# Five steps for a tile, and a second half of whole turns: the order of the later tiles and of the weights in a two-half mixture of experts

## The chip, the cores and the metric

One core of one Trainium2 chip. The metric is the time of one execution on the device in microseconds, the median of three runs. 1 per cent of it is 2.66 us.

## The reference

The input `x` has 16 sequences of 64 tokens with 256 channels: 1024 tokens. The layer norm of `x` gives the keys of a recurrent attention, the context gives its values. A scan over each sequence keeps a sum of exp(key) times value and a sum of exp(key), both decayed by channel; their quotient is added to `x`. Then the layer norm of that goes through a mixture of 32 experts, each of which computes `(silu(h @ w_gate) * (h @ w_up)) @ w_down` with 96 inner channels. Every token goes to the 8 experts of the largest probability, with these 8 weights divided by their sum. An expert takes at most 512 pairs, counted in the order of the tokens; later ones are dropped.

```python
x = x + wkv(w, u, layernorm(x), ctx)
h = layernorm(x)
probs = softmax(h @ gate_w); w, sel = top_k(probs, 8); w = w / w.sum(-1)
y[e] = (silu(h @ w_gate[e]) * (h @ w_up[e])) @ w_down[e]
x = x + sum over the chosen e of w * y[e]      # at most 512 pairs per expert
```

## The kernel before

All experts are computed for all tokens, and the routing weight is multiplied in (zero where an expert isn't chosen). To keep float32 accuracy, each operand is split into a high and a low part (`whi`, `wlo`, `h_hi`, `h_lo`, `t_hi`, `t_lo`), and three products of them are summed.

The tokens are eight tiles of 128. The first half of the work takes tiles 0 to 3, the second half tiles 4 to 7. Each half goes over all 32 experts in 8 groups of four. A group has three steps (`GT`), a step being 128 rows of the inner dimension. Two groups are a pair and make a turn of six steps; there are four turns in a half. Weights lie in two slots (`raw`, `whi`, `wlo`), one for each group of a pair.

A step `n` on TensorE (`turn`, from L753) is in this order: `project` of the up product of step n (L712, 6 matmuls); at the first step of a group the routing weights for the group's rows (`weights`, L719); `project` of the gate of step n+1; then whatever the dictionary `beside` has for this step; the down product of step n-1 (`down`, L733, 12 matmuls of 256 columns in a whole step); then whatever `after` has. TensorE takes these strictly in order. ScalarE's `step` (L562) makes `s_sb = silu(gate)`, does the stages that stand `between`, and rounds `t_hi` from `t_sb`; after each step it makes one part of `whi` of the group that comes next in that slot (`split_high`, L537). VectorE's `step` (L1069) makes `t1 = w * s` and `t = up * t1`, and then has stages of its own. POOL makes `t_lo = t - t_hi` (`product_low`, L402), then its stages, then one part of `wlo` (`split_low`, L373). Every queue is in order, so a stage that waits holds what stands behind it.

In the first turn of each half the tokens aren't all ready, so that turn has two passes with 256 columns each: 12 half-width steps instead of 6 whole ones. All other turns are whole (512 columns).

The attention, the norm and the routing of tiles 0 to 3 are done before and in the first turn. Each tile of 4 to 7 (units 2 to 5) goes through beside the steps of the first half's turns, by six steps per tile (`later_turn`): while the front of one unit (norm of x, `turn_kv`, `exps`, the scans in `all_sums`, `fractions_and_inverse`, `mix`, `turn_mixed`) is under way, the back of the unit before it is too (`add_mixed`, its norm, `turn_h`, `take_h`, `h_low`, `keep_low`, `logits`, `largest`, `route_exps`, `choose`, `ranks`, `weigh`, `turn_parts`, `take_route`). `take_h` (L508, L510) and `keep_low` (L386) put a tile's `h_hi` and `h_lo` in place. The back of the last unit falls into the 256-column passes of the second half's first turn, whose first pass only needs tiles 4 and 5. On ScalarE the exponentials and the Silu have different tables; `fetch_silu` (L529) brings Silu's back ahead of the next step.

SP loads the raw weights of a group when both splits of the one before it in the slot are done (`reload`, L321 to L327), and with each pair the context tile of the next unit (`load_context`, L316). The second half loads all eight groups again, in the same order. The outputs of a half are added on VectorE (`add_output`, L1102) and the next sums started on TensorE (`start_sum`, L751).

`keep_clock` (L748) multiplies zeros into a bank that nobody reads, to keep TensorE active where it waits; there are several in the start-up, one of them with three matmuls ahead of the first `turn_parts`.

## Time and profile before

| | us |
|---|---|
| median of the runs | 265.92 |
| range of three runs | 265.85 to 268.53 |
| the profiled execution, its own time | 266.44 |
| its span | 264.7 |
| TensorE busy in it | 242.0 (91%) |
| VectorE, ScalarE, POOL busy | 138.0, 138.1, 162.9 |
| mean granted clock of TensorE | 0.981 |

The span is the part that the profile covers; the execution's own time lies 1.74 us above it. Busy times of TensorE are modelled with the pipeline's depth: a matmul of 512 columns shows some 0.40 us and follows the one before it by 0.23. Where the text counts work of TensorE, it therefore takes distances between starts, not durations.

### The profile page before, as it was taken

How to read it: one execution, taken by the hardware profiler on the slowest of the kernel's cores; microseconds unless marked ns; L12 is line 12 of the kernel's file. 1: busy time of each engine (PE TensorE's matmuls, PEld its weight loads, DVE VectorE, ACT ScalarE, POOL GpSimd, SP SyncE). 2: the span in 40 equal slices, each digit the busy share in tenths (PEclk: the TensorE clock that was granted, in tenths of full speed). 3: DMA queues.
4: the chain of work that ended last, by engine and by line, in shares of the span. 5: the costliest groups of instructions: out<-in, count | busy, mean ns of one | idle time of the engine just before them, and what ended most of it. 6: DMA issues, size and time to landing. Idle time of an engine off the chain costs nothing.

```text
span 264.7 us, 4893 instructions
## 1 busy us (share of the span) xinstructions
PE 242.0 (91%) x1479; PEld 206.3 (78%) x1483; DVE 138.0 (52%) x361; ACT 138.1 (52%) x263; POOL 162.9 (62%) x152
## 2 busy tenths in 40 slices
PE   6366999899999999999999887999999999999993
PEld 1324889797788887887888787997888888888883
DVE  4698666673528853495529854532432323233333
ACT  2875657444666536844776367335535253534420
POOL 5128551349785757684975876339686767767630
PEclk9959799999999999999999999999999999999999
DMA  6940661000505141241505052400515050700002
GB/s 194 265 134 28 174 173 33 2 1 4 152 26 143 58 125 55 62 139 28 150 2 158 20 148 73 143 0 0 143 39 161 21 165 13 229 30 1 0 2 79
DMA packets 43367, 22.34 MB, mean 84 GB/s; under 512 B 34129, under 2 KB 43345, under 8 KB 43345
## 3 DMA queue, kind: packets, MB, share of 16 engines
q1 hardware_dynamic: 42496, 21.63, 28.3%
q10 hardware_dynamic: 848, 0.43, 0.6%
q8 instruction: 12, 0.20, 0.3%
q14 instruction: 11, 0.08, 0.1%
HBM read 21.01 MB, written 1.05 MB: 83 GB/s over the span
## 4 chain that ended last, share of the span: by engine, by line
PE 64%; DVE 13%; issue 9%; POOL 6%; ACT 5%; DMA 1%; DVEq 0%; POOLq 0%; ACTq 0%
PE bank L712 36%; PE bank L733 21%; DVE t_sb L1075 3%; PE bank L670 2%; POOL wlo L373 2%; DVE t_sb L1081 2%; DVE inv L950 2%; DVE bank L939 2%; POOL rstd L381 2%; PE bank L719 1%; POOL t_lo L402 1%; ACT normed L478 1%; PE bank L638 1%; DMA x_sb<-in_x_dram 1%; ACT t_hi L572 1%
## 5 line engine op out<-in xcount | busy, mean ns | idle before, releaser
L402 POOL TENSOR_TENSOR t_lo<-t_sb,t_hi 128x512 fp32r<-128x512 f32 (+1 forms) x59 | 63.0, 1067 | 73.3 <-ACT t_hi L572 69.6
L373 POOL TENSOR_TENSOR wlo<-raw,whi 128x768 fp32r<-128x768 f32 x48 | 88.3, 1842 | 13.6 <-ACT whi L537 13.4
L712 PE MATMUL bank<-h_hi,whi 128*128 128x512 f32 (+1 forms) x240 | 89.3, 372 | 1.3 <-DVE t_sb L1081 0.5
L712 PE MATMUL bank<-h_hi,wlo 128*128 128x512 f32 (+1 forms) x240 | 84.4, 352 | 0.0
L712 PE MATMUL bank<-h_lo,whi 128*128 128x512 f32 (+1 forms) x240 | 84.4, 351 | 0.0
L1075 DVE TENSOR_TENSOR t_sb<-bank,s_sb 128x512 f32<-128x512 f32 (+1 forms) x60 | 35.0, 583 | 92.2 <-PE bank L719 46.9
L572 ACT ACTIVATE t_hi<-t_sb 128x512 fp32r<-128x512 f32 (+1 forms) x60 | 32.7, 545 | 92.7 <-DVE t_sb L1081 92.6
L712 PEld LDWEIGHTS bank<-h_hi,whi 128*128 128x128 f32 x240 | 46.1, 192 | 6.8 <-issue 1.5
L712 PEld LDWEIGHTS bank<-h_hi,wlo 128*128 128x128 f32 x240 | 45.7, 190 | 6.6
L733 PE MATMUL bank<-whi,t_hi 128*128 128x256 f32 x192 | 50.1, 291 | 0.7 <-ACT t_hi L572 0.7
L712 PEld LDWEIGHTS bank<-h_lo,whi 128*128 128x128 f32 x240 | 45.9, 191 | 4.7
L733 PE MATMUL bank<-wlo,t_hi 128*128 128x256 f32 x192 | 48.3, 282 | 0.0
L537 ACT ACTIVATE whi<-raw 128x768 fp32r<-128x768 f32 x48 | 39.9, 835 | 8.5 <-PE bank L733 7.2
L1081 DVE TENSOR_TENSOR t_sb<-bank,t_sb 128x512 f32<-128x512 f32 (+1 forms) x60 | 35.1, 585 | 11.0 <-PE bank L712 8.3
L733 PEld LDWEIGHTS bank<-whi,t_hi 128*128 128x128 f32 x192 | 36.4, 190 | 2.4 <-ACT t_hi L572 1.1
L733 PEld LDWEIGHTS bank<-wlo,t_hi 128*128 128x128 f32 x192 | 36.4, 189 | 1.3
L733 PE MATMUL bank<-whi,t_lo 128*128 128x256 f32 x192 | 33.0, 284 | 0.1
L567 ACT ACTIVATE s_sb<-bank 128x512 f32<-128x512 f32 (+1 forms) x60 | 29.6, 494 | 0.0
L733 PEld LDWEIGHTS bank<-whi,t_lo 128*128 128x128 f32 x192 | 27.2, 191 | 0.3 <-POOL t_lo L402 0.3
L748 PE MATMUL bank<-zeros_bf 128*128 128x512 bf16 x30 | 10.6, 508 | 5.0 <-POOL ident L357 2.6
L748 PEld LDWEIGHTS bank<-zeros_bf 128*128 128x128 bf16 x31 | 3.6, 125 | 9.8 <-issue 3.7
L912 DVE TENSOR_TENSOR_SCAN state<-factors,bank 128x256 f32<-128x256 f32 (+1 forms) x12 | 9.8, 850 | 0.0
(112 smaller groups left out, 187.5 us busy)
## 6 DMA issues: line engine op xcount, KB each, us to landing
raw<-in_L_ffn_w_gate_dram SPq DMA_DIRECT2D x16, 384.0 KB
raw<-in_L_ffn_w_up_dram SPq DMA_DIRECT2D x16, 384.0 KB
raw<-in_L_ffn_w_down_dram SPq DMA_DIRECT2D x48, 128.0 KB
out_dram<-x SPq DMA_DIRECT2D x4, 256.0 KB, 2.5
x_sb<-in_x_dram SPq DMA_DIRECT2D x1, 512.0 KB, 6.8
ctx_tile<-in_ctx_dram SPq DMA_DIRECT2D x4, 128.0 KB, 5.3
x_sb<-in_x_dram SPq DMA_DIRECT2D x1, 256.0 KB, 3.6
ctx_sb<-in_ctx_dram SPq DMA_DIRECT2D x1, 256.0 KB, 4.7
```

The lines of the kernel that those rows point to most:

```text
L373: pool.tensor_tensor(split_view(wlo, slot, part), raw_parts(slot, part), split_view(whi, slot, part).bitcast(F32), ALU.subtract).then_inc( ...
L381: chain.link(pool.tensor_tensor(rstd[row][:], var[row][:], neg_half[:, 0:u.tiles], ALU.pow))
L402: pool.tensor_tensor(t_lo[k % 2][:, c], t_sb[:, c], t_hi[k % 2][:, c].bitcast(F32), ALU.subtract).then_inc(t_lo_ready, 1)
L537: nc.scalar.activation(split_view(whi, slot, part), raw_parts(slot, part), ACT.Copy).then_inc(w_hi_ready, 1)
L567: nc.scalar.activation(s_sb[:, c], g_ps(k)[:, c], ACT.Silu).then_inc(s_ready, 1)
L572: nc.scalar.activation(t_hi[k % 2][:, c], t_sb[:, c], ACT.Copy).then_inc(t_hi_ready, 1)
L712: last = nc.tensor.matmul(ps[:, c], up_weight(w, slot, part, k, j), h[:, k, tokens], start=(i == 0), stop=(i == len(terms) - 1))
L733: return nc.tensor.matmul(y_tile(t), a[odd][:, at:at + P], down_weight(b, slot, j), start=False, stop=stop)
L748: nc.tensor.matmul(ps[:], zeros_bf[:, 0:P], zeros_bf[:], start=(i == 0), stop=(i == count - 1))
L912: return chain.add(nc.vector.tensor_tensor_scan(flat(state[s][:, i]), flat(by_decay), flat((num_ps, den_ps)[i][s]), 0.0, ALU.mult, ALU.add))
L1075: nc.vector.tensor_tensor(t1_sb[:, c], w_ps[:, c], s_sb[:, c], ALU.mult).then_inc(t1_ready, 1)
L1081: nc.vector.tensor_tensor(t_sb[:, c], u_ps(k)[:, c], t1_sb[:, c], ALU.mult).then_inc(t_ready, 1)
```

## The change

- The later units come every five steps (`CYCLE`) instead of six, counted from the first whole turn of the first half. `cycle(it, k)` gives the place `at` in the cycle (0 to 4), the unit whose back is due, and the one whose front is due. With 18 whole steps in the first half, the three cycles with a front take steps 0 to 14, and the last unit's back takes steps 15 to 17. Within a cycle, `turn_kv`, `logits`, `turn_mixed` and `turn_parts` stand behind the down product; `turn_h` and `ranks` stay ahead of it. `route_exps` now comes ahead of `exps`.
- The second half has four whole turns, no passes: 24 steps instead of 30. TensorE waits for `h_hi_kept` (a new semaphore of `take_h`) and `h_lo_kept` of all four tiles ahead of the second half's first gate product, in step 17 of the first half's whole turns.
- The second half takes the pairs in reverse, so the pair of the last turn of the first half stays in its slots: that pair isn't loaded and split again.
- The output of the first half is added in one stage after the second half's first step; both sums start in its second step.
- Loops on the other engines that carried the later tiles are written out. `begin_sums` waits for `keys_ready` ahead of its first write for a later tile.
- Three matmuls of `keep_clock` ahead of the first `turn_parts` are gone.

```diff
+        def cycle(it, k):
+            n, at = divmod((it - 1) * TURN_STEPS + k, CYCLE)
+            n += LATER[0]
+            return at, later(n), later_routed(n), later(n + 1) if n + 1 in LATER else None
...
-        ALL_STEPS = 2 * HALF_STEPS
+        FIRST_STEPS = GROUPS * GT + TURN_STEPS
+        ALL_STEPS = FIRST_STEPS + GROUPS * GT
+        CYCLE = 5
...
+        def pair_before(half, it):
+            return it + half * (TURNS - 1)
+        def first_group(half, it):
+            return (TURNS - 1 - it) * 2 if half else it * 2
...
@@ SP @@
-                done = it * 6 + (half * GROUPS + slot + 1) * 3
+                done = pair_before(half, it) * 6 + (slot + 1) * 3
...
-                load(slot, group)
+                load(slot, first_group(half, it + 1) + slot)
...
-                if half == 0:
-                    for slot in range(2):
-                        reload(half, slot, TURNS - 1, slot)
...
@@ POOL: tiles are called behind product_low of the step @@
+            def tiles_beside(it, k):
+                at, back, _, front = cycle(it, k)
+                if at == 0:
+                    power(back, back.second_norm)
+                    if front:
+                        power(front, front.first_norm)
+                elif at == 2:
+                    keep_low(back)
+            for it in range(1, TURNS):
+                turn(0, it, WHOLE, tiles=tiles_beside, split=(1, 2) if it < TURNS - 1 else (1,))
+            turn(1, 0, WHOLE, split=(2,))
...
@@ ScalarE: tiles are called between the step's Silu and its t_hi @@
+            def tiles_beside(it, k):
+                at, back, routed, front = cycle(it, k)
+                if at == 0 and back.n > LATER[0]:
+                    take_route(later_routed(back.n - 1))
+                elif at == 1:
+                    norm_h(back)
+                    if front:
+                        norm_x(front)
+                elif at == 2:
+                    take_h(back)
+                    route_exps(routed)
+                    if front:
+                        exps(front)
+                    fetch_silu(back.n - 1)
...
@@ TensorE @@
                         elif half == 0 and it == TURNS - 1:
-                            pe.wait_ge(h_lo_kept, NT)
-                            project(n + 1, 1, 0, 0, 0, 0, GROUPS)
+                            pe.wait_ge(h_hi_kept, HT)
+                            pe.wait_ge(h_lo_kept, HT)
+                            project(n + 1, 1, None, 0, 0, 0, group)
...
+                        if half and first_turn and k == 1:
+                            pe.wait_ge(out_ready, 2)
+                            for m in range(HT // NT):
+                                start_sum(m)
...
-            keep_clock(3, h_ps[0])
             turn_parts(first_routed)
...
+            def tiles_beside(it, k):
+                at, back, routed, front = cycle(it, k)
+                if at == 1:
+                    turn_h(back)
+                elif at == (3 if front else 2):
+                    ranks(routed)
+            def tiles_after(it, k):
+                at, back, routed, front = cycle(it, k)
+                if at == 1:
+                    if front:
+                        turn_kv(front)
+                    logits(routed)
+                elif at == (4 if front else 2):
+                    if front:
+                        turn_mixed(front)
+                    turn_parts(routed)
...
@@ VectorE @@
+                if s == 2:
+                    dve.wait_ge(keys_ready, u.n + 1)
...
+            def tiles_beside(it, k):
+                at, back, routed, front = cycle(it, k)
+                if at == 0:
+                    add_mixed(back)
+                    if front:
+                        stats_x(front)
+                elif at == 1:
+                    h_low(back)
+                    largest(routed)
+                elif at == 2:
+                    choose(routed)
+                    if front:
+                        all_sums(front)
+                    else:
+                        weigh(routed)
+                elif at == 3:
+                    fractions_and_inverse(front)
+                elif at == 4:
+                    mix(front)
+                    weigh(routed)
...
+            turn(1, 0, WHOLE, {(0, 0): [(first_output, 0), (first_output, 1)]})
```

## Rows read from the trace of the kernel before

**Rows 1.** Chain that ended last, shares of the span by engine (page, part 4)
```profile
PE 64%; DVE 13%; issue 9%; POOL 6%; ACT 5%; DMA 1%; DVEq 0%; POOLq 0%; ACTq 0%
```

**Rows 2.** Timeline, PE, weights matmuls: start us, us, instruction [idle before <-releaser]
```profile
64.97 0.39 PE L719 MATMUL bank<-route,spread 96*128 96x512 bf16 x1
...
93.86 0.39 PE L719 MATMUL bank<-route,spread 96*128 96x512 bf16 x1
...
123.04 0.39 PE L719 MATMUL bank<-route,spread 96*128 96x512 bf16 x1
...
210.02 0.39 PE L719 MATMUL bank<-route,spread 96*128 96x512 bf16 x1
...
235.86 0.39 PE L719 MATMUL bank<-route,spread 96*128 96x512 bf16 x1
```

**Rows 3.** Chain in order of time: start us, us, what
```profile
26.50 2.62 PE bank L712 x12
...
181.39 1.87 POOL wlo L373
...
198.90 1.43 PE bank L733 x12
...
200.33 2.79 PE bank L712 x12
```

**Rows 4.** Timeline, PE, rows with idle time before them, 70 to 160 us
```profile
70.58 0.51 PE L653 MATMUL bank<-ident,normed 128*128 128x128 f32 x2 [0.29 <-ACT normed L478]
...
100.58 0.50 PE L629 MATMUL bank<-ident,normed 128*128 128x128 f32 x2 [0.47 <-ACT normed L478]
...
119.83 0.44 PE L638 MATMUL bank<-ident,mixed 128*128 128x128 f32 x2 [0.41 <-DVE mixed L978]
...
159.51 0.26 PE L670 MATMUL bank<-gate_hi,tile_hi 128*128 128x32 f32 x1 [1.14 <-DVE tile_lo L997]
```

**Rows 5.** Timeline, PE keep_clock and DVE's last part of weigh, 24 to 42 us
```profile
30.57 0.82 PE L748 MATMUL bank<-zeros_bf 128*128 128x512 bf16 x3
...
29.99 0.23 DVE L1039 TENSOR_TENSOR parts<-bank,parts 128x64 bf16<-128x64 f32 x1
```

**Rows 6.** Timeline, SP's queue, context tile of the last unit
```profile
113.42 0.34 SPq L319 DMA_DIRECT2D ctx_tile<-in_ctx_dram  x1
```

**Rows 7.** DMA issues (page, part 6): KB each, median us to landing
```profile
ctx_tile<-in_ctx_dram SPq DMA_DIRECT2D x4, 128.0 KB, 5.3
```

**Rows 8.** Timeline, ACT take_h and DVE h_low, 64 to 76 us
```profile
72.98 0.37 ACT L508 ACTIVATE tile_hi<-bank 128x256 fp32r<-128x256 f32 x1
...
75.67 0.41 DVE L997 TENSOR_TENSOR tile_lo<-bank,tile_hi 128x256 fp32r<-128x256 f32 x1
```

**Rows 9.** Timeline, DVE, choose to the end of weigh, turn 2
```profile
110.77 0.19 DVE L1010 MAX8 top<-bank 128x8 f32<-128x32 f32 x1
...
121.03 0.19 DVE L1039 TENSOR_TENSOR parts<-bank,parts 128x32 bf16<-128x32 f32 x1
```

**Rows 10.** Timeline: gate on PE, then t, t_lo, keep_low of one step, turn 2
```profile
103.99 0.40 PE L712 MATMUL bank<-h_hi,whi 128*128 128x512 f32 x1
...
104.25 0.69 DVE L1081 TENSOR_TENSOR t_sb<-bank,t_sb 128x512 f32<-128x512 f32 x1 [1.20 <-PE bank L712]
...
105.68 1.28 POOL L402 TENSOR_TENSOR t_lo<-t_sb,t_hi 128x512 fp32r<-128x512 f32 x1 [1.30 <-ACT t_hi L572]
...
106.91 0.40 POOL L386 CAST h_lo<-tile_lo 128x256 f32 x1
```

**Rows 11.** Timeline, ACT's table load and DVE's maximum, 41 to 64 us
```profile
41.59 1.28 ACT L517 ACT_TABLE_LOAD   x1
...
41.72 0.22 DVE L1002 TENSOR_REDUCE neg_max<-bank 128x2 f32<-128x64 f32 x1 [0.88 <-PE bank L670]
```

**Rows 12.** Windows of 1 us: PE, PEld, DVE, ACT, POOL busy, PEclk, DMA share, GB/s
```profile
24.00:25.00 1.00, 0.00 (x0) 0.01 (x1) 0.81 (x2) 0.88 (x2) 0.98 (x2) 1.00 0.00 0
...
26.00:27.00 1.00, 1.00 (x8) 1.00 (x8) 0.60 (x3) 0.13 (x1) 0.78 (x1) 0.76 0.28 43
```

More of the change, by code:

```diff
@@ L402, in product_low, with turn @@
                 pool.tensor_tensor(t_lo[k % 2][:, c], t_sb[:, c], t_hi[k % 2][:, c].bitcast(F32), ALU.subtract).then_inc(t_lo_ready, 1)
-            def turn(half, it, passes, beside={}, split=(1, 2), leave_last=False):
+            def turn(half, it, passes, beside={}, split=(1, 2), leave_last=False, tiles=None):
                 for p in passes:
@@ L560, in _, with step @@
                 split_high(1, part, 1)
-            def step(n, k, p, between=()):
+            def step(n, k, p, between=(), tiles=None):
                 c = columns(p)
@@ L572, in step, with turn @@
                 nc.scalar.activation(t_hi[k % 2][:, c], t_sb[:, c], ACT.Copy).then_inc(t_hi_ready, 1)
[L574 removed]
+            def turn(half, it, passes, beside={}, split=(1, 2), tiles=None):
                 for p in passes:
                     for k in range(TURN_STEPS):
[L577 removed]
+                        step(steps_before(half, it) + (p or 0) * TURN_STEPS + k, k, p, beside.get((p or 0, k), []), tiles and (lambda: tiles(it, k)))
                         ahead = k // GT + 1
                         if ahead in split and p in (None, ahead - 1):
[L580 to L590 removed]
+                            split_high(ahead % 2, k % GT, pair_before(half, it) * 2 + ahead, steps_of_last_user(half, it, ahead))
+            third = later(2)
             turn(0, 0, PASSES, {(0, 0): [lambda: take_route(first_routed)],
@@ L595, in _ @@
                                 (0, 5): [lambda: take_route(second_routed)]}, split=(2,))
[L596 to L602 removed]
+            def tiles_beside(it, k):
[12 more added lines that the diff above has]
+                    fetch_silu(back.n - 1)
+            for it in range(1, TURNS):
+                turn(0, it, WHOLE, tiles=tiles_beside, split=(1, 2) if it < TURNS - 1 else (1,))
+            turn(1, 0, WHOLE, {(0, 0): [lambda: take_route(later_routed(LATER[-1]))]}, split=(2,))
             with act.Fori(1, TURNS - 1) as it:
@@ L796, in turn @@
                             down(n - 1, 0, 1, GT - 1, 1, None)
-                        elif not first_turn:
-                            down(n - 1, 1 if it == 1 else None, 1, GT - 1, 1, None)
+                        elif half or not first_turn:
+                            down(n - 1, 1 if half == 0 and it == 1 else None, 1, GT - 1, 1, None, last=half == 1 and first_turn)
                         for stage in after.get((p or 0, k), []):
                             stage()
-            def later_turn(it):
-                back, front, routed = later(it + 1), later(it + 2), later_routed(it + 1)
-                turn(0, it, WHOLE, {(0, 1): [lambda: turn_h(back), lambda: turn_kv(front)],
-                                    (0, 2): [lambda: logits(routed)],
-                                    (0, 5): [lambda: turn_mixed(front)]},
-                     {(0, 3): [lambda: ranks(routed)], (0, 5): [lambda: turn_parts(routed)]})
+                        if tiles:
+                            tiles[1](it, k)
             pe.sem_inc(down_done, 2)
@@ L824, in _ @@
             project(1, 0, 0, 0, 0, 1, 0)
[L825 removed]
             turn_parts(first_routed)
[L828 removed]
+            third = later(2)
             turn(0, 0, PASSES, {(0, 3): [lambda: logits(second_routed)],
@@ L834, in _ @@
                  {(0, 2): [lambda: turn_h(second)]})
+            def tiles_beside(it, k):
[14 more added lines that the diff above has]
+                    turn_parts(routed)
             for it in range(1, TURNS):
-                later_turn(it)
-            down(HALF_STEPS - 1, None, 1, GT - 1, 1, None, last=True)
-            turn(1, 0, PASSES, {(0, 1): [lambda: turn_h(last)], (0, 2): [lambda: logits(last_routed)]},
-                 {(0, 3): [lambda: ranks(last_routed)], (0, 5): [lambda: turn_parts(last_routed)]})
+                turn(0, it, WHOLE, tiles=(tiles_beside, tiles_after))
+            turn(1, 0, WHOLE)
             for it in range(1, TURNS - 1):
@@ L1081, in step, with turn @@
                 nc.vector.tensor_tensor(t_sb[:, c], u_ps(k)[:, c], t1_sb[:, c], ALU.mult).then_inc(t_ready, 1)
-            def turn(half, it, passes, beside={}):
+            def turn(half, it, passes, beside={}, tiles=None):
                 for p in passes:
@@ L1089, in turn @@
                             stage(u)
-            def later_turn(it):
-                back, front, routed = later(it + 1), later(it + 2), later_routed(it + 1)
-                turn(0, it, WHOLE, {(0, 0): [(add_mixed, back), (stats_x, front)],
-                                    (0, 2): [(h_low, back), (largest, routed)],
-                                    (0, 3): [(choose, routed), (all_sums, front)],
-                                    (0, 4): [(fractions_and_inverse, front)],
-                                    (0, 5): [(mix, front), (weigh, routed)]})
+                        if tiles:
+                            tiles(it, k)
             def add_output(half, q):
```

106 lines of the change are left out of this document (37 added, 69 removed).

## The prediction

> **What bounds the kernel now.** I read the chain of waits first. Most of it is TensorE [rows 1], so a change is worth what it does to TensorE's order and to the places where TensorE stands still. The second view is the timeline of TensorE cut at the `weights` matmul (L719) with which each turn begins [rows 2]. From 210.02 to 235.86 a whole turn of the second half takes 25.84 us, and the other later turns repeat this: TensorE never waits there. A step is up and gate (2.79) and down (1.43) [rows 3], and a `weights` matmul comes every third step. From 93.86 to 123.04 a turn of the first half with a tile beside it takes 29.18, so a tile costs 3.34. The third view is the idle time of TensorE [rows 4]: 0.47 and 0.41 of those 3.34 are waits (for `norm_x`, for `mix`), and the remaining 2.46 is matmul work for the tile. Near the half boundary the waits are longer: 1.14 before the last tile's logits at 159.5, and three more of 0.3 to 1.1. The half-width steps of the second half's first turn add another kind: where POOL has a 128x768 split of 1.87 [rows 3] and a `t_lo` in a half-width step of about 2.1, TensorE is held by POOL.
>
> **The change part by part.** I count from the first whole turn (64.97) to the third turn of the second half (210.02): 145.05 now [rows 2].
>
> (1) Work that must remain. Five clean turns are 5 x 25.84 = 129.20. The first begins with a half-width down, half of 1.43 [rows 3]: -0.72. Three tiles with back and front are 3 x 2.46 = 7.4. The last tile has no front; half of 2.46, an estimate, is 1.2. The two matmuls that start the new sums are about 0.3. Sum 137.4. So 145.05 - 137.4 = 7.7 us of today's stretch are waits and restarts: tiles in three turns, the late `mix` before the boundary, the last tile in half-width steps, POOL in those steps. Turning 12 half-width steps into 6 whole ones saves next to nothing in columns (a half-width down is 6 matmuls for 12); it only takes away the POOL limit. All 7.7 are open to removal; what follows is what is late next.
>
> (2) The three `keep_clock` matmuls before the first `turn_parts` go. They take 30.57 to about 31.2, and the parts were ready at 30.2 [rows 5]. ScalarE's `take_route` and the first `weights` wait behind them, so the chain starts 0.66 earlier: -0.66. Bounds: 0 to -0.66; I take the latter, as nothing from outside the chain ends there.
>
> (3) The reverse order takes away the reload of one pair, six splits on ScalarE and six on POOL. None of it ends a wait of a whole turn (POOL has a split and a `t_lo` in a step of 4.2 us), so 0. The loads that now follow come earlier and are hidden. On SP the context tile for the last unit is issued behind the same reload as now, 113.42, that is 19.6 after its turn's mark, and lands 5.3 later [rows 6, 7]. It was used a turn later; now it is used in that turn's sixth step, after five steps, gate, down and the tiles' work: about 27.9 after the mark. With the splits about 1 us later it lands near 26: hidden, by 2 us. If not, TensorE waits in `turn_kv`, between 0 and about 2 us.
>
> (4) Five steps per tile. DVE, ScalarE and POOL keep the same sequence, less the empty step between `norm_h` and `h_low`. The wait of `norm_x` (0.3 to 0.5) goes, because `turn_kv` now stands behind the down; that of `mix` (0.4) goes for the same reason. In their place come two. Logits: in turn 1 `turn_h` starts at 70.58 [rows 4]; with turning (0.25), down (1.43) and `turn_kv` (0.6) logits could start at 72.85. But `take_h` ends at 73.35 and `h_low` takes 0.41 [rows 8]: ready 73.8, wait 0.95. ScalarE is late since `norm_x`, `t_hi` and a split stand before that step's Silu. For the second tile I get about 0.7, and for the third, whose steps have no `weights` matmul to hold DVE, 0.15: 1.8 in all. While `h_low` and `largest` wait, DVE's next t1 is queued behind them; TensorE needs its product only a step later, so nothing more is lost. Parts: today `choose` to the end of `weigh` takes 110.77 to 121.2 [rows 9], 10.4 us; with the new start (0.95 after the up of its step) I get parts 0.2 to 0.35 after TensorE asks for them: 0.8 for three tiles. `turn_h` of the first tile waits as now, 0.3. The added wait for `keys_ready` in `begin_sums` is met while `choose` runs (1.3): 0. Sum of (4): 2.9; bounds 0.5 (all met in time) to 4.5.
>
> (5) The boundary. The last step of the first half (step 17 of the whole turns) is the last tile's third. TensorE does its up and then waits for `h_lo_kept` of all four tiles before the second half's first gate. POOL does that `keep_low` only behind `t_lo` of the very same step, which needs `t_hi`, which needs t, which needs the up that has just ended. Such a chain stands in the trace: t starts at 104.25, t_lo at 105.68, `keep_low` at 106.91 and it ends at 107.3 [rows 10]. The up before it gave way to the gate at 104.0, so 3.3, and 0.1 for the semaphore: 3.4 us with nothing for TensorE to do, for the down of step 16 and `ranks` stand behind the waiting gate. ScalarE must also do `take_h`, `route_exps`, a return to Silu and two table loads of 1.28 ahead of this `t_hi`. The load does not wait for the maximum: one began at 41.59, when `neg_max` began at 41.72 [rows 11]. By that it is done just before t is: 3.4 stays. Bounds: 3.3 to 4.6 (a load behind the maximum adds about 1.1). Behind it `turn_parts` waits for `weigh`, 0.1. `out_ready` is asked for a step later than the outputs are added (1.4 us to spare): 0.
>
> On (5) the Trainium skill (ScalarE: Activation LUTs, What ACT_TABLE_LOAD costs) has a drain of about 1.38 us beside each load's 1.28. The load at 41.59 starts 0.02 after ScalarE's Silu and is followed at once, so the trace does not agree; with it the two loads would put the `t_hi` some 2.6 later.
>
> (6) The clock. It fell from the upper level (2.4 GHz) to the lower (1.2 GHz) in the microsecond from 26, after TensorE had done nothing from 24 to 25 and small matmuls since [rows 12]. Twelve half-width matmuls then took 2.62, where twelve of the same width take 1.43 [rows 3]: 1.2 us lost, perhaps 1.4 to the end of that spell. Since 30 us TensorE never stood still for over 1.14 us [rows 4] and the clock was full. A pause of 3.4 us is three times as long as either, though dense work stands on both sides. I take it that the clock falls there: 1.3, less 0.1 of waiting that it hides: +1.2. Bounds 0 and 2.4 (twice the spell).
>
> Sum: -7.7 - 0.66 + 2.9 + 3.4 + 0.1 + 1.2 = -0.8 us. The profiled execution took 266.44 (span 264.7), 0.52 over the median of 265.92. Against the median: 265.1 us.
>
> **Rivals.** A, the clock holds. For it: nothing below 1.2 us of idle touched the clock after 30 us, and the work around is dense. Against: the spell at 26. Then -2.0: 263.9. The Trainium skill, TensorE: Matmul & The Clock Gate, HAM oscillation, says that a gap between bursts of matmuls can send the clock down each time; by it A falls, and the trace shows such a fall only after sparse work.
>
> B, five steps are enough for the tiles: logits and parts are ready in time, since ScalarE and DVE shift by more than I count. For it: today's `turn_parts` never waits. Against: the walk of [rows 8, 9]. Then (4) costs 0.5 and the clock decides the rest: 261.5 to 262.7, say 262.4.
>
> C, slower: ScalarE's queue in step 17 becomes what ends the boundary wait. Its place is `t_hi` behind two loads, `route_exps` (which waits for logits, already late) and the return to Silu. By my count it ends only 0.1 before t is ready. Each microsecond more is a microsecond on TensorE; from 0.8 us on the change loses. A load behind the maximum gives 1.1: 266.2; late logits as well, up to 2.5: 267.6. For it: the slack of 0.1. Against: the load at 41.59. By the page's drain it would be 267.7.
>
> D, the first part: without `keep_clock` the clock falls again at 31; a spell such as that at 26 takes back the 0.66 and 0.7 more: 266.5. Against it stands the short pause, about 1 us.
>
> **How the numbers follow.** Forecast 0.45, A 0.27, B 0.11, C 0.12, D 0.05. The range must hold 0.8: from the middle of B to nearly the end of C, 262.4 to 267.2. One per cent is 2.66 us, about what a measurement of this kernel can tell from no change: faster means under 263.3, slower over 268.6. Under 263.3 lie B whole and some 0.10 of A: 0.21. Over 268.6 lies only C with a second fall or a tile wait that I missed: 0.08. The rest, 0.71, is no change that can be told.
>
> **What would show it.** One idle stretch of TensorE of 3.4 us ended by POOL's cast at the end of the first half, near 148 us, and a granted clock at the lower level for about 3 us behind it. Small waits in each tile's cycle before logits (up to 1 us) and before the parts, none for `mixed` or `norm_x`. The first `weights` matmul near 31.3 instead of 31.98. Turns of 25.84 through the whole second half, the first one included. Wrong would be: a boundary pause under 2 us, or one ended by an activation long after t is there, or waits in the tile cycles that add up to over 4.5 us.

## The result, and the profile after

| | before | after |
|---|---|---|
| median of 20 runs each, us | 266.31 | 268.50 |
| range, us | 265.50 to 268.70 | 266.90 to 269.73 |
| the profiled execution, its own time | 266.44 | 268.78 |
| its span | 264.7 | 267.0 |
| mean granted clock of TensorE | 0.981 | 0.968 |

The ratio of after to before is 1.0049 (1.0027 to 1.0071): the change makes the kernel slightly slower. The forecast was 265.1 with a range to 267.2, so it was wrong, by 3.4 us and in its sign. Some 0.4 of that is the base: the forecast started from 265.92, the median of three runs of before, which is 266.31 over twenty. Against the profiled execution of before, the sum said 265.64 for one that took 268.78. One run of x1_split (1298.01 us), one of x4_fillb (475.56) and one of the kernel before beside them (1298.37) stand far outside all others and are left out of every median and ratio below.

The chain of waits of after, its shares by engine from the page, answers to [rows 1]. TensorE's share has grown and POOL's has shrunk, as a second half without half-width steps should have it.

```profile
PE 72%; DVE 11%; issue 7%; ACT 3%; DMA 3%; POOL 2%; ACTq 1%; DVEq 0%; POOLq 0%
```

The second view is the timeline of TensorE in after. The `weights` matmuls (now L742) answer to [rows 2], the rows with idle time before them to [rows 4]; up and gate are now L735, the down is L756.

```profile
64.60 0.39 PE L742 MATMUL bank<-route,spread 96*128 96x512 bf16 x1
...
73.33 0.25 PE L693 MATMUL bank<-gate_hi,tile_hi 128*128 128x32 f32 x1 [0.95 <-DVE tile_lo L1036]
...
87.97 0.26 PE L716 MATMUL bank<-ident_bf,parts 128*96 128x128 bf16 x1 [0.43 <-DVE parts L1078]
...
99.53 0.25 PE L693 MATMUL bank<-gate_hi,tile_hi 128*128 128x32 f32 x1 [1.82 <-DVE tile_lo L1036]
...
115.58 0.26 PE L716 MATMUL bank<-ident_bf,parts 128*96 128x128 bf16 x1 [0.28 <-DVE parts L1078]
...
139.49 0.26 PE L716 MATMUL bank<-ident_bf,parts 128*96 128x128 bf16 x1 [0.23 <-DVE parts L1078]
...
154.13 0.47 PE L735 MATMUL bank<-h_hi,whi 128*128 128x512 f32 x1 [3.23 <-issue]
...
186.50 0.39 PE L742 MATMUL bank<-route,spread 96*128 96x512 bf16 x1
...
212.34 0.39 PE L742 MATMUL bank<-route,spread 96*128 96x512 bf16 x1
...
238.18 0.39 PE L742 MATMUL bank<-route,spread 96*128 96x512 bf16 x1
```

The stretch that the prediction counted, from the first whole turn to the third turn of the second half, runs from 64.60 to 212.34: 147.74 us, where before took 145.05 and the forecast comes to 144.95 (145.05 less 0.1: its sum without the 0.66 that lies ahead of the stretch). The rows say where 147.74 go: 2.77 us of waits for `tile_lo` (0.95 and 1.82, none for the third tile), 0.94 for the parts (0.43, 0.28, 0.23), and a pause of 3.23 at the half boundary (the profile has no engine for its end and writes "issue"; the views of POOL below show what ends it). Less these 6.94, 140.8 are left for work that was put at 137.4. The second half's turns are clean: 186.50 to 212.34 and on to 238.18 is 25.84 each, as before; the first one, from 160.22 to 186.50, takes 26.28.

Of these 140.8 and 137.4, the difference of 3.4 us shows in part in the chain in order of time. Twelve `project` matmuls take 2.79 there wherever the clock is full, and a whole down 1.43 [rows 3]; two places of after stand out.

```profile
100.43 4.36 PE bank L735 x12
...
106.22 2.79 PE bank L735 x12
...
150.91 3.23 issue
154.13 2.39 PE bank L735 x6
156.60 2.26 PE bank L756 x12
```

The windows of 1 us say why (PE, PEld, DVE, ACT and POOL busy with their instructions, then the granted clock, the DMA share and GB/s). In this stretch of after the clock goes from the upper level (2.4 GHz) to the lower (1.2 GHz) at two places: just behind the 1.82 us that TensorE waited for `tile_lo`, and behind the 3.23 us at the boundary.

```profile
99.00:100.00 1.00, 0.47 (x5) 0.51 (x5) 0.38 (x1) 0.98 (x2) 1.00 (x1) 1.00 1.17 325
100.00:101.00 1.00, 1.00 (x6) 0.90 (x6) 0.53 (x2) 0.98 (x3) 0.04 (x1) 0.56 0.57 170
...
102.00:103.00 1.00, 1.00 (x4) 0.71 (x4) 0.00 (x0) 1.00 (x1) 0.00 (x0) 0.50 0.27 96
...
104.00:105.00 1.00, 1.00 (x8) 0.86 (x7) 0.79 (x7) 1.00 (x2) 0.30 (x1) 1.00 0.13 45
...
153.00:154.00 1.00, 0.00 (x0) 0.00 (x0) 0.00 (x0) 0.00 (x0) 1.00 (x2) 1.00 0.00 0
...
155.00:156.00 1.00, 1.00 (x4) 0.66 (x2) 0.00 (x0) 0.00 (x0) 0.00 (x0) 0.50 0.00 0
```

The fall at the boundary was in the forecast; the one at 100 was not, and the wait ahead of it is more than twice the 0.7 that was worked out for it. To see what holds the second tile's `tile_lo`, the timeline of ScalarE in that step:

```profile
95.64 0.63 ACT L592 ACTIVATE t_hi<-t_sb 128x512 fp32r<-128x512 f32 x1 [0.90 <-DVE t_sb L1118]
...
97.32 0.84 ACT L555 ACTIVATE whi<-raw 128x768 fp32r<-128x768 f32 x1 [1.05 <-PE bank L756]
98.07 0.58 ACT L585 ACTIVATE s_sb<-bank 128x512 f32<-128x512 f32 x1
98.55 0.38 ACT L526 ACTIVATE tile_hi<-bank 128x256 fp32r<-128x256 f32 x1
```

ScalarE is done with `t_hi` at 96.27. Next in its queue is a `split_high`, which overwrites a part of `whi` and so waits for a down product of TensorE: 1.05 us. Silu and `take_h` are queued behind that split, DVE's `h_low` needs `take_h`, and TensorE's logits need `h_low`. So a product that TensorE has just done releases a chain on which TensorE then waits. The working of the prediction counted how long this split takes, not that it waits.

At the boundary the views of DVE, ScalarE and POOL show the chain that was forecast, t, `t_hi`, `t_lo` and `keep_low` [rows 10], and the table loads [rows 11] out of its way:

```profile
149.45 0.19 DVE L1041 TENSOR_REDUCE neg_max<-bank 128x1 f32<-128x32 f32 x1 [0.99 <-PE bank L693]
...
151.00 0.69 DVE L1118 TENSOR_TENSOR t_sb<-bank,t_sb 128x512 f32<-128x512 f32 x1 [0.75 <-PE bank L735]
```

```profile
148.46 1.28 ACT L535 ACT_TABLE_LOAD   x1
149.76 0.26 ACT L535 ACTIVATE bank<-bank,neg_max 128x32 f32<-128x32 f32 x1
150.04 1.28 ACT L547 ACT_TABLE_LOAD   x1
...
151.72 0.63 ACT L592 ACTIVATE t_hi<-t_sb 128x512 fp32r<-128x512 f32 x1 [0.18 <-DVE t_sb L1118]
```

```profile
152.43 1.26 POOL L417 TENSOR_TENSOR t_lo<-t_sb,t_hi 128x512 fp32r<-128x512 f32 x1 [3.92 <-ACT t_hi L592]
153.63 0.40 POOL L401 CAST h_lo<-tile_lo 128x256 fp32r<-128x256 f32 x1
```

`t_hi` waits for t alone. POOL's cast ends at 154.03, and TensorE goes on at 154.13. The first load begins at 148.46, a microsecond ahead of the maximum that the exponential behind it needs.

### The profile page after: what moved, and what is told of

The parts are those of the page before. It is cut to its first block, busy times and chain, and to the rows that moved or that the text cites. A ratio compares the mean times of both kernels' runs of the same rounds, so it can differ in the third digit from the quotient of the medians.

```text
span 267.0 us, 4296 instructions
## 1 busy us (share of the span) xinstructions
PE 243.3 (91%) x1403; PEld 203.1 (76%) x1406; DVE 136.0 (51%) x349; ACT 132.7 (50%) x242; POOL 151.2 (57%) x140
## 3 DMA queue, kind: packets, MB, share of 16 engines
HBM read 18.65 MB, written 1.05 MB: 74 GB/s over the span
## 4 chain that ended last, share of the span: by engine, by line
PE 72%; DVE 11%; issue 7%; ACT 3%; DMA 3%; POOL 2%; ACTq 1%; DVEq 0%; POOLq 0%
PE bank L735 44%; PE bank L756 22%; DMA ctx_sb<-in_ctx_dram 3%; PE bank L693 2%; DVE t_sb L1118 1%; PE bank L742 1%; DVE t_sb L1112 1%; DVE bank L978 1%; ACT s_sb L585 1%; DVE mixed L1017 1%; POOL t_lo L417 1%; ACT t_hi L592 1%; POOL wlo L388 1%; DVE inv L989 1%; POOL rstd L396 1%
## 5 line engine op out<-in xcount | busy, mean ns | idle before, releaser
L735 PE MATMUL bank<-h_hi,whi 128*128 128x512 f32 (+1 forms) x216 | 85.6, 396 | 3.9 <-issue 3.2
L388 POOL TENSOR_TENSOR wlo<-raw,whi 128x768 fp32r<-128x768 f32 x42 | 77.3, 1843 | 13.6 <-ACT whi L555 13.3
L735 PE MATMUL bank<-h_hi,wlo 128*128 128x512 f32 (+1 forms) x216 | 80.7, 374 | 0.0
L735 PE MATMUL bank<-h_lo,whi 128*128 128x512 f32 (+1 forms) x216 | 80.4, 372 | 0.0
L592 ACT ACTIVATE t_hi<-t_sb 128x512 fp32r<-128x512 f32 (+1 forms) x54 | 31.5, 584 | 94.8 <-DVE t_sb L1118 94.5
L756 PE MATMUL bank<-whi,t_hi 128*128 128x256 f32 x192 | 50.3, 293 | 0.7 <-ACT t_hi L592 0.7
L735 PEld LDWEIGHTS bank<-h_hi,whi 128*128 128x128 f32 x216 | 41.5, 192 | 10.0 <-issue 4.0
L756 PE MATMUL bank<-wlo,t_hi 128*128 128x256 f32 x192 | 48.6, 284 | 0.0
L735 PEld LDWEIGHTS bank<-h_hi,wlo 128*128 128x128 f32 x216 | 41.1, 190 | 7.9
L735 PEld LDWEIGHTS bank<-h_lo,whi 128*128 128x128 f32 x216 | 41.4, 192 | 5.5
L555 ACT ACTIVATE whi<-raw 128x768 fp32r<-128x768 f32 x42 | 34.9, 835 | 8.5 <-PE bank L756 8.3
L756 PEld LDWEIGHTS bank<-whi,t_hi 128*128 128x128 f32 x192 | 36.9, 192 | 2.7 <-ACT t_hi L592 1.1
L756 PEld LDWEIGHTS bank<-wlo,t_hi 128*128 128x128 f32 x192 | 37.0, 193 | 1.5
L756 PE MATMUL bank<-whi,t_lo 128*128 128x256 f32 x192 | 32.1, 284 | 0.1
L756 PEld LDWEIGHTS bank<-whi,t_lo 128*128 128x128 f32 x192 | 26.9, 192 | 0.3 <-POOL t_lo L417 0.3
L396 POOL TENSOR_TENSOR rstd<-var,neg_half 128x1 f32<-128x1 f32 (+1 forms) x12 | 7.1, 596 | 5.4 <-DVE var L915 5.4
```

Source lines behind the costliest of these rows:

```text
L388: pool.tensor_tensor(split_view(wlo, slot, part), raw_parts(slot, part), split_view(whi, slot, part).bitcast(F32), ALU.subtract).then_inc( ...
L396: chain.link(pool.tensor_tensor(rstd[row][:], var[row][:], neg_half[:, 0:u.tiles], ALU.pow))
L555: nc.scalar.activation(split_view(whi, slot, part), raw_parts(slot, part), ACT.Copy).then_inc(w_hi_ready, 1)
L592: nc.scalar.activation(t_hi[k % 2][:, c], t_sb[:, c], ACT.Copy).then_inc(t_hi_ready, 1)
L735: last = nc.tensor.matmul(ps[:, c], up_weight(w, slot, part, k, j), h[:, k, tokens], start=(i == 0), stop=(i == len(terms) - 1))
L756: return nc.tensor.matmul(y_tile(t), a[odd][:, at:at + P], down_weight(b, slot, j), start=False, stop=stop)
```

## The experiments

The theory from these rows: the loss against the forecast is a wait mid-queue on ScalarE and a second fall of the clock that comes of it; the boundary is as forecast. The rivals: the fall is a matter of the transfers at 99 to 100 (a DMA share of 1.17 there), not of the wait; the boundary pause has another cause than `keep_low` behind its step's `t_lo`; or the steps of the change that were costed at 0 are what lost the time. Each ratio is to the kernel before, run on the same chip beside it.

**x1_split.** ScalarE does the split of step 6 (the one above) behind `take_h` of the next step. Nothing else is changed in the kernel after.

```diff
@@ ScalarE turn @@
+                        if tiles and it == 2 and k == 0:
+                            late.append(lambda: split_high(1, 0, ...))
-                        if ahead in split and p in (None, ahead - 1):
+                        elif ahead in split and p in (None, ahead - 1):
...
@@ ScalarE tiles_beside, at == 2 @@
                     take_h(back)
+                    if late:
+                        late.pop()()
                     route_exps(routed)
```

> One edit to the changed kernel: ScalarE does the weight split of step 6 (the first step of the second whole turn) behind the next step's take_h instead of ahead of its Silu. Theory: in the changed kernel this split waits for the down product of step 6 (1.05 us) with Silu and take_h queued behind it, so TensorE waits 1.82 us for the logits and its clock falls for some 3 us. Then the wait before these logits shrinks to under 0.4 us, the granted clock stays at 1.00 around 100 us, and the profiled time falls by 2.5 to 3.2 us, against the changed kernel's 268.8, to about 265.9. The pause at the half boundary and the low clock behind it stay. Rival: the five-step cycle is too short for VectorE and ScalarE as a whole; then the wait only moves to the parts or to the next logits and the time falls by under 1 us.

Median 266.07, ratio 0.9952 (0.9919 to 0.9986). The profiled execution took 266.14, 2.64 less than after and so within what was expected, and the stretch takes 145.40, 2.34 less than after. No row with idle time stands before these logits any more. The timeline of ScalarE in x1_split shows the order turned round, and its window of TensorE holds the full clock:

```profile
95.30 0.63 ACT L594 ACTIVATE t_hi<-t_sb 128x512 fp32r<-128x512 f32 x1 [0.89 <-DVE t_sb L1124]
95.84 0.58 ACT L587 ACTIVATE s_sb<-bank 128x512 f32<-128x512 f32 x1
96.32 0.38 ACT L526 ACTIVATE tile_hi<-bank 128x256 fp32r<-128x256 f32 x1
...
97.05 0.83 ACT L555 ACTIVATE whi<-raw 128x768 fp32r<-128x768 f32 x1
```

```profile
99.00:100.00 1.00, 1.00 (x6) 0.82 (x5) 0.30 (x1) 0.99 (x5) 0.80 (x1) 1.00 1.08 301
100.00:101.00 1.00, 1.00 (x7) 0.82 (x6) 0.83 (x5) 0.98 (x3) 0.00 (x0) 1.00 0.28 92
...
149.00:150.00 1.00, 0.00 (x0) 0.00 (x0) 0.09 (x1) 0.00 (x0) 1.00 (x2) 0.70 0.00 0
...
155.00:156.00 1.00, 1.00 (x8) 0.98 (x6) 0.02 (x1) 0.00 (x0) 0.00 (x0) 0.50 0.00 0
```

One instruction's place in the queue was worth the 1.82 us and the fall behind it, and the kernel is now a little faster than before. The transfers at 99 are about as busy as in after (1.08 against 1.17; in x3_both 1.17, with the clock at 1.00), so they aren't what lets the clock down. At the boundary the pause is as it was, 3.22. But here the clock falls while TensorE still waits, in the microsecond after 149, and stays low to that after 156; in after it was low from 154 to 158. So the gain is larger than the 2.34 shows. From the `weights` at 93.43 to the next `weights` it is 14.63, where after takes 18.08 for the same: 3.45 come back at the edit, and the longer spell at the boundary takes 1.13 of them away (137.30 to 157.58, against 141.07 to 160.22 in after).

**x2_keep.** POOL does `keep_low` of the last tile ahead of that step's `product_low`, not behind it.

```diff
@@ POOL turn, ahead of product_low @@
+                        if tiles and it == TURNS - 1 and k == TURN_STEPS - 1:
+                            keep_low(later(LATER[-1]))
...
@@ POOL tiles_beside @@
-                elif at == 2:
+                elif at == 2 and front:
                     keep_low(back)
```

> One edit to the changed kernel: for the last tile POOL does keep_low ahead of that step's t_lo instead of behind it. Theory: the pause of 3.23 us at the half boundary is POOL's order alone (t, t_hi, t_lo, keep_low), and the low clock behind it follows from the pause. Then TensorE goes on with the second half's first gate at once, waits some 0.6 us for the mask before ranks, the clock stays at 1.00 there, and the profiled time falls by 3.2 to 4.2 us to about 265.0. Rival: ScalarE's copy of h_hi or the stages behind it end as late as POOL does; then the pause stays over 2 us and the time falls by under 1.5 us.

Median 264.05, ratio 0.9896 (0.9839 to 0.9954). The stretch takes 143.93, 3.81 less than after: 3.23 for the pause and about 1.1 for the clock, less a new wait of 0.60. What was behind the pause is late in its place, by the timeline of TensorE in x2_keep: `ranks` waits for `choose`, at 152.57.

```profile
152.57 0.19 PE L711 MATMUL bank<-mask,earlier 128*128 128x32 bf16 x1 [0.60 <-DVE bank L1060]
```

The clock stays full from 148 to 159. The wait of 1.82 at 99.21 and the fall from 100 to 103.8 are still there: each loss stands without the other, this one here and the boundary's in x1_split.

**x3_both.** Both edits.

> Both edits together. Theory: the two losses are separate and add: 268.8 less 2.9 and 3.7 gives about 262.2 us in the profile, 1.4 to 1.9 per cent under the kernel before, with the clock at 1.00 from 30 us on. Rival: once both pauses are gone, another wait of the tile cycles takes their place and the gains don't add: 264 us or more.

Median 261.61, ratio 0.9812 (0.9774 to 0.9850). The stretch takes 140.49, 7.25 less than after: 3.46 at the second tile and 3.79 at the boundary, as with each edit by itself (3.45 and 3.78). The granted clock is 1.00 from 31 us until TensorE's last work is done. TensorE waits 2.7 us in it (0.94 for the first tile's `tile_lo`, 0.60 before `ranks`, 1.14 for the parts of four tiles), so 137.8 are left: the work that the prediction put at 137.4 was 0.4 too little. Run once more as **y3**, beside two others:

> The kernel with both edits (split of step 6 and keep_low) once more, as the base of the next one on the same chip: 261.6 within 0.4.

Median 261.50, ratio 0.9807 (0.9767 to 0.9848), the stretch 140.51: the same.

**x4_fillb.** The wait of the boundary stays, and TensorE multiplies zeros into a free bank while it lasts (`keep_clock` takes the bank as an argument here).

```diff
                         elif half == 0 and it == TURNS - 1:
+                            keep_clock(14, bank[5])
                             pe.wait_ge(h_hi_kept, HT)
```

> One edit to the changed kernel: fourteen matmuls of zeros (512 columns) into a bank that is free then, ahead of TensorE's wait at the half boundary. The pause stays as long (POOL still ends it), but TensorE is active in it. Theory: the low clock behind the pause comes from the pause; then the clock stays at 1.00 there and the profiled time falls by 1.0 to 1.6 us to about 267.5; the fall near 100 us stays. Rival: the clock falls there all the same, and the time stays within 0.4 us of 268.8 or grows.

No lower clock at the boundary, and the stretch takes 145.11, but the times have two levels: five runs at 265.85 to 266.37 and four at 267.86 to 268.03 (median of the nine 266.37, ratio 1.0004, 0.9969 to 1.0038). The profiled execution is of the lower one. The fall near 100 was expected to stay; in this execution the wait of 1.82 at 99.53 stands as in after but no fall follows; this is the window of x4_fillb that answers to that of after:

```profile
100.00:101.00 1.00, 1.00 (x8) 0.86 (x8) 0.62 (x2) 0.99 (x3) 0.05 (x1) 1.00 0.54 163
```

So the pause of 1.82 lets the clock fall in some executions (after, x2_keep) and not in others. From the `weights` at 93.76 to the same instruction 16.53 us later in x4_fillb, 18.08 in after: one such fall costs 1.55 us. If that is the whole of the two levels, filling this pause too should leave one.

**x5_fillbl.** x4_fillb, and eight matmuls of zeros ahead of those logits.

```diff
@@ TensorE tiles_after, at == 1 @@
+                    if it == 2 and k == 0:
+                        pe.wait_ge(s_ready, steps_before(0, it) + k + 1)
+                        keep_clock(8, u_ps(k + 1))
                     logits(routed)
```

> The changed kernel with matmuls of zeros in both pauses: fourteen ahead of the wait at the half boundary and eight ahead of the logits of the second whole turn's first step. Both pauses stay as long. With the boundary filled alone, half of the runs took about 266.2 and half about 267.9. Theory: these two levels are the clock's fall near 100 us, which comes in some executions and not in others after the pause of 1.82 us. Then all runs lie near 266.2 (265.8 to 266.6), and the clock is at 1.00 from 32 us on. Rival: the two levels have another cause, for the kernel before has runs near 266.0 and near 268.0 as well; then both levels remain.

Ten runs, all within 265.70 to 266.59; median 266.26, ratio 0.9960 (0.9933 to 0.9988), and a stretch of 145.11 in the profiled execution. Its clock is full at both places; this is the window of x5_fillbl at the boundary:

```profile
155.00:156.00 1.00, 0.99 (x9) 0.78 (x7) 0.83 (x5) 0.04 (x1) 0.00 (x0) 1.00 0.03 8
```

Its mean clock of 0.999 is not the zeros' work alone, since the spell of lower clock in the start-up (from 11 to 21 us in after) is missing too; other runs of x5_fillbl have 0.968 to 0.981 and the same times. Both waits stand at full length, since zeros only pass the time. So the clock alone is worth 2.63 us of after's stretch (147.74 less 145.11), 1.55 of it at 100 and 1.1 at the boundary, and 2.2 us of its median (268.50, measured apart from these runs).

**b_fill.** The kernel before, with six matmuls of zeros where it waits 1.14 for the last tile's logits.

```diff
@@ TensorE of the kernel before @@
+            def fill():
+                pe.wait_ge(s_ready, steps_before(1, 0) + 3)
+                keep_clock(6, u_ps(3))
...
-            turn(1, 0, PASSES, {(0, 1): [lambda: turn_h(last)], (0, 2): [lambda: logits(last_routed)]},
+            turn(1, 0, PASSES, {(0, 1): [lambda: turn_h(last)], (0, 2): [fill, lambda: logits(last_routed)]},
```

> The kernel before with six matmuls of zeros (512 columns) ahead of the last tile's logits, where TensorE waits 1.14 us at 159.5. Theory: the kernel before has two levels (about 266.0 and 268.0) because this pause and the one of 0.7 us behind it let the clock fall in some executions; then its runs come to the lower level, 265.7 to 266.8, and the median is 0.3 to 1.5 below that of the kernel before in the same call. Rival: the levels have another cause (the start-up); then both levels remain.

Twelve runs within 265.56 to 266.92, where the kernel before had 5 of 17 above 267 beside it. The medians are 266.14 and 266.30 (0.9983, 0.9955 to 1.0011): no difference that can be told. That the upper runs of before come from this pause fits, but no profile of such a run is there, so it isn't shown.

**x6_kc.** x3_both with the three `keep_clock` matmuls back ahead of the first `turn_parts`; **y6** is the same again, beside y3.

```diff
+            keep_clock(3, h_ps[0])
             turn_parts(first_routed)
```

> The kernel with both edits (split and keep_low), and the three keep_clock matmuls ahead of the first turn_parts put back. Theory: they hold the chain by 0.66 us, so the time is 0.5 to 0.8 above 261.6, about 262.3. Rival: without them the clock stays low longer in the start-up, and they cost nothing or even save: 261.6 or less.

> The same with the three keep_clock matmuls ahead of the first turn_parts. The first measurement gave 262.1 against 261.6, in different runs. Theory: 0.4 to 0.8 above its base of the same call, and 0.6 to 0.75 more between the first logits and the first weights matmul in the trace. Rival: within 0.2 of its base.

x6_kc: 262.11 (0.9803, 0.9767 to 0.9839). y6: 261.18 (0.9795, 0.9754 to 0.9837). x3_both and y3 without them: 261.61 and 261.50. The times don't tell them apart, and the 0.4 to 0.8 that y6 was expected to lose against y3 did not come. The traces say why: it hangs on whether the clock fell between 26 and 28. Where it did, from the first logits to the first `weights` is 6.96 (before), 7.01 (x6_kc) and 6.95 (y6) with these matmuls and 6.29 (x1_split, x3_both) without: 0.66. Where it held, 6.02 with (b_fill) and 6.03 without (y3, after), as the parts end the wait either way. This stays at 0 to 0.66 by the execution. The rows of y6 (the clock fell, and the zeros end the wait) and of y3 (it held, and the parts do) show two of these cases:

```profile
31.31 0.82 PE L779 MATMUL bank<-zeros_bf 128*128 128x512 bf16 x3
32.72 0.28 PE L750 MATMUL bank<-route,spread 96*128 96x256 bf16 x1 [0.47 <-ACT route L544]
```

```profile
30.43 0.31 PE L724 MATMUL bank<-ident_bf,parts 128*96 128x128 bf16 x2 [1.08 <-DVE parts L1086]
31.21 0.28 PE L750 MATMUL bank<-route,spread 96*128 96x256 bf16 x1 [0.47 <-ACT route L544]
```

**x7_fwd.** x3_both with the second half in forward order: the first pair is loaded and split again beside the last turn of the first half.

```diff
         def pair_before(half, it):
-            return it + half * (TURNS - 1)
+            return it + half * TURNS
         def first_group(half, it):
-            return (TURNS - 1 - it) * 2 if half else it * 2
+            return it * 2
...
@@ SP, with the last turn of the first half @@
+                if half == 0:
+                    for slot in range(2):
...
+                        load(slot, slot)
...
@@ POOL and ScalarE @@
-                turn(0, it, WHOLE, tiles=tiles_beside, split=(1, 2) if it < TURNS - 1 else (1,))
+                turn(0, it, WHOLE, tiles=tiles_beside, split=(1, 2))
```

> The kernel with both edits, but the second half takes the pairs in the order of the first half, so that the first pair is loaded and split again at the boundary. Prediction's part 3: the reverse order is worth nothing in itself, 261.6 plus or minus 0.3. Rival: the splits now stand in ScalarE's and POOL's queues in steps 15 to 17, ahead of the last tile's take_h and keep_low, as they do in the second tile; then TensorE waits 0.5 to 1.5 us for the last logits or for h_lo_kept, with a fall of the clock up to 3 us more: 262.1 to 264.5.

Median 263.54, ratio 0.9855 (0.9816 to 0.9894): the rival is right. The stretch takes 142.73, 2.24 more than x3_both, in an execution that is the slowest of six (three lie from 263.94 to 264.10, three from 262.49 to 263.15). With the splits of steps 15 and 16 in ScalarE's queue, the last tile's logits wait, and the clock falls behind them. The timeline of ScalarE in x7_fwd, the same steps in x3_both, and then the timeline of TensorE and a window of x7_fwd:

```profile
141.34 0.85 ACT L562 ACTIVATE whi<-raw 128x768 fp32r<-128x768 f32 x1 [0.82 <-PE bank L769]
...
144.22 0.63 ACT L601 ACTIVATE t_hi<-t_sb 128x512 fp32r<-128x512 f32 x1 [0.91 <-DVE t_sb L1131]
144.76 0.83 ACT L562 ACTIVATE whi<-raw 128x768 fp32r<-128x768 f32 x1
145.50 0.57 ACT L594 ACTIVATE s_sb<-bank 128x512 f32<-128x512 f32 x1
145.97 0.37 ACT L533 ACTIVATE tile_hi<-bank 128x256 fp32r<-128x256 f32 x1
```

```profile
143.12 0.63 ACT L596 ACTIVATE t_hi<-t_sb 128x512 fp32r<-128x512 f32 x1
143.74 0.60 ACT L589 ACTIVATE s_sb<-bank 128x512 f32<-128x512 f32 x1
144.23 0.38 ACT L528 ACTIVATE tile_hi<-bank 128x256 fp32r<-128x256 f32 x1
```

```profile
146.95 0.25 PE L706 MATMUL bank<-gate_hi,tile_hi 128*128 128x32 f32 x1 [1.25 <-DVE tile_lo L1049]
```

```profile
149.00:150.00 1.00, 1.00 (x4) 0.81 (x3) 0.30 (x1) 0.87 (x2) 0.00 (x0) 0.50 0.00 0
```

From `t_hi` to `take_h` it is 1.75 us with the split and 1.11 without. The split before that one waits 0.82 for TensorE and makes Silu, and with it t and `t_hi`, late: `t_hi` by 0.75, counted from the turn's first `weights`. The reverse order is worth 1.4 to 2.2 us here (1.43 between the medians of x7_fwd and x6_kc, run beside each other; 2.24 of the stretch). The rows put that down to the splits that no longer stand ahead of a tile's `take_h`; no wait in them is ended by the transfers that the reverse order saves.

**x8_all.** x3_both's rule for every tile: in the step with `take_h` to come, the split goes behind it.

```diff
-                        if tiles and it == 2 and k == 0:
+                        if tiles and ahead in split and cycle(it, k)[0] == 1:
                             late.append(...)
```

> The kernel with both edits, and the split behind take_h in each tile's cycle, not in the second tile's alone. Theory: the wait of 0.94 us before the first tile's logits (near 73 us) is the same kind, a split of 0.83 in ScalarE's queue ahead of Silu and take_h; it shrinks to 0.3 or less, and the time falls by 0.5 to 0.8 us to about 261.0. Rival: there Silu waits for norm_x and t_hi, not for the split; then the wait stays over 0.6 us and the time within 0.3 us of 261.6.

Median 260.71, ratio 0.9758 (0.9723 to 0.9794); the stretch takes 139.60, 0.89 less than x3_both. The first tile's wait of 0.94 goes down to 0.22, by the timeline of TensorE in x8_all:

```profile
71.91 0.25 PE L701 MATMUL bank<-gate_hi,tile_hi 128*128 128x32 f32 x1 [0.22 <-DVE tile_lo L1044]
```

This is the best version of the study, 2.4% under the kernel before. It keeps the whole of the change and moves a cast on POOL and three splits on ScalarE.

## Why the prediction was wrong

Its mechanism at the boundary was right. What failed is the walk of the second tile, in size, and the clock, which fell once more than was counted.

(1) Work that must remain. 137.4 was 0.4 short: x3_both leaves 137.8 and x8_all 137.6 (139.60 less 1.97 of waits). The POOL limit is gone as forecast, and the second half's first turn shows no wait of its own; it takes 26.28, so the start of the new sums costs 0.44, where 0.3 was put.

(2) `keep_clock`. -0.66 holds only where the clock fell between 26 and 28. In after it held there, and the first logits came 0.56 later than before (25.58 against 25.02), so the first `weights` stands at 31.61, not at 31.3; the stretch begins 0.37 earlier than before. What the removal is worth on the median is open: x6_kc, y6, x3_both and y3 don't tell.

(3) The reverse order was put at 0, "None of it ends a wait of a whole turn". That was wrong: x7_fwd shows 2.24 us of stretch in its profiled execution, since the splits that it saves stand in ScalarE's queue ahead of `take_h`. The step looked for splits that end a wait on TensorE themselves, and not for chains with a split in the middle. The sum didn't suffer: the change takes the pairs in reverse, and in after the last tile's logits don't wait.

(4) Five steps. The waits of `norm_x` and `mix` are gone, as said. The first tile's logits wait 0.95 as worked out, the third's 0 instead of 0.15, the parts 0.94 instead of 0.8, and `turn_h` 0 instead of 0.3. But "for the second tile I get about 0.7" was 1.82: this is the step that failed first. The 5-step cycle puts the second tile's `take_h` behind a `split_high` that waits 1.05 for TensorE's down product, while the first tile's split starts right behind `t_hi` (at 71.15 in after, with no wait). The working has a split ahead of Silu, but not what a split itself may wait for. x1_split shows it by its order alone.

(5) The boundary. 3.23 was measured for 3.4 by the row of idle time, which begins at the modelled end of a matmul; by starts, as the prediction counts, it is 3.39 (150.51 to 154.13, less the 0.23 of a matmul). It is ended by the cast on POOL, with both table loads out of the way, and x2_keep shows this by POOL's order alone. Rival C did not come about. By the Trainium skill (ScalarE: Activation LUTs, What ACT_TABLE_LOAD costs) about 1.38 us of drain belong to each load; the trace after does not agree, as the load that ends at 149.74 is followed by the exponential at 149.76 and by the next load at 150.04.

(6) The clock. At the boundary it fell, for 1.1 us by x5_fillbl, where 1.2 was said; that this came so near is in part luck, as the same pause cost 2.2 in x1_split (20.28 from 137.30 to 157.58, against 18.08 in x5_fillbl). The argument that nothing under 1.2 us of idle touched it was sound as far as it went, but its sum held a single pause over that, because step (4) had put the other at 0.7. With 1.82 there, a second fall came in the profiled execution: 1.55 us. Two errors in one: the wait was mis-sized, and the fall hung on it.

The differences, from forecast to the profiled stretch: second fall +1.55, logits +1.0 (2.77 for 1.8), work +0.4, parts +0.1, `turn_h` -0.3, the clock and the wait behind the boundary -0.2, the pause 0 by starts. They sum to 2.5, and 147.74 less 144.95 is 2.8; 0.3 is not put down to a row. Ahead of the stretch 0.3 more is missing, 0.37 for 0.66.

The rivals: A (the clock holds) is wrong by the windows, and what it would have given is about x5_fillbl's 266.26, not 263.9, as the waits that it took over from the forecast were too short. B is wrong; x8_all, with five steps, is where the tiles come near to it (1.15 us for the parts and 0.22 for logits, where B had 0.5 in all), and beats its 262.4 only because the boundary is mended as well. D did not come about in the profiled execution. The 8 in 100 for the slower side named "a second fall or a tile wait that I missed". Both came, but they were too cheap to be seen as a slowdown of over 1%.

## What to carry to other kernels

When the alignment of a periodic job to the loop is changed, walk every engine's queue anew for each of its instances, and count for what stands ahead not only how long it takes but what it waits for: a refill that waits for the engine that in turn waits for this queue costs more than it lasts. Where work at a phase's end gates the other engine, look for the one short instruction of it (here a cast of 0.40 us) and put it ahead of the long product that it doesn't need. A pause in dense TensorE work should be priced with the clock that may fall behind it; matmuls of zeros tell the two apart, and a reorder that removes the pause gets both.

## What the runs showed of the hardware

A pause of 1.82 us in otherwise dense work, with 32-column matmuls just behind it, let the clock down in after and x2_keep and not in x4_fillb; one of 1.25 us did so in x7_fwd. That fall cost nearly as much as the pause itself (1.55 for 1.82); behind the pause of 3.2 us it cost 1.1 in after and 2.2 in x1_split. Matmuls of zeros held the clock through each pause in which they were tried (x4_fillb, x5_fillbl). By the Trainium skill (TensorE: Matmul & The Clock Gate, HAM oscillation) the waits for transfers between the bursts of matmuls of one kernel sent the clock down on every tile. The pause of 3.2 us agrees, in both profiles that left it empty (after, x1_split); the pause of 1.82 did so in two of three.

After as such has runs from 266.90 to 269.73. Six of the 20 lie within 266.90 to 267.17 and twelve above 268.2, about a fall's worth apart, and x5_fillbl, where neither pause is left empty, has one level. So one and the same program differs by over 1.5 us between executions, and that this hangs on whether the clock falls fits x4_fillb and x5_fillbl. It is not shown for single runs: no run of after's lower group was profiled, and none of x4_fillb's upper one. A run's mean clock doesn't tell, as the start-up moves it without moving the time (in x5_fillbl 0.971 at 266.20 and 0.999 at 266.32).
